# Count tiles of a graph convolution built in two row tiles of the TensorE array, two slots at a time

## The reference, cut to what matters

```python
deg_out = jnp.maximum(jax.ops.segment_sum(ones, src, num_segments=N), 1.0)
deg_in = jnp.maximum(jax.ops.segment_sum(ones, dst, num_segments=N), 1.0)
h = x * jax.lax.rsqrt(deg_out)[:, None]
agg = jax.ops.segment_sum(h[src], dst, num_segments=N)
h = agg * jax.lax.rsqrt(deg_in)[:, None]
h = jax.nn.relu(h @ W + b)
gnn = h / jnp.maximum(jnp.linalg.norm(h, axis=1, keepdims=True), EPS)
x = x + gnn + mix(xn)
x = x + ffn(layernorm(x))      # 8 experts, top 1, capacity 1.25
```

## Time and profile before

| | us |
|---|---|
| median of 3 runs | 1531.53 (1530.54 to 1535.5) |
| the profiled execution | 1529.9 |
| its span in the trace | 1528.7 |
| TensorE busy | 1394.8 |
| VectorE busy | 1304.5 |
| ScalarE busy | 925.8 |
| GpSimd busy | 709.4 |

### The profile page before, as it was taken

One profiled execution on the slowest core, in us unless ns is written; L12 is line 12 of the kernel. 1 busy time (PEld: TensorE's weight loads), 2 busy tenths in 40 slices (PEclk: granted clock), 3 DMA queues, 4 the chain that ended last, 5 costly groups with the idle time before them and its releaser, 6 DMA issues. The chain is left out here.

```text
span 1528.7 us, 37659 instructions
## 1 busy us (share of the span) xinstructions
PE 1394.8 (91%) x11633; PEld 970.7 (63%) x11634; DVE 1304.5 (85%) x2630; ACT 925.8 (61%) x2090; POOL 709.4 (46%) x740
## 2 busy tenths in 40 slices
PE   3899999896889999999999999999996699899985
PEld 3666666674546666666666666666664588889985
DVE  7999998899768999999999999999995577857774
ACT  4456655567446667666666666666663566555653
POOL 4578776506212443244323442244321567776575
PEclk9899999998899999999999999999998799999998
DMA  9011111000001100011111100110113333243220
GB/s 295 30 33 41 40 39 37 29 21 28 2 4 50 54 34 34 34 69 34 34 34 61 42 34 34 36 67 34 34 35 130 121 109 120 95 136 105 82 69 17
DMA packets 61417, 89.46 MB, mean 59 GB/s; under 512 B 10411, under 2 KB 40749, under 8 KB 61312
## 3 DMA queue, kind: packets, MB, share of 16 engines
q1 hardware_dynamic: 49999, 67.18, 13.0%
q0 software_dynamic: 11328, 21.23, 4.9%
HBM read 62.89 MB, written 35.01 MB: 64 GB/s over the span
## 5 line engine op out<-in xcount | busy, mean ns | idle before, releaser
L1453 PE MATMUL bank<-reg_b,reg_a 128*128 128x512 f16 x2401 | 637.5, 379 | 0.7 <-ACT reg_a L1087 0.7
L1087 ACT ACTIVATE reg_a<-bank 128x392 f16<-128x392 f32 x784 | 370.4, 496 | 219.9 <-PE bank L1447 218.5
L1662 DVE TENSOR_TENSOR reg_c<-iota_v,reg_c 128x2048 f16<-128x2048 f16 (+2 forms) x398 | 422.9, 1085 | 30.3 <-PE bank L1447 22.9
L782 POOL COPY key_deg<-deg_k 128x1 f32 (+1 forms) x49 | 93.8, 1914 | 463.2 <-DVE reg_c L1793 463.2
L1447 PEld LDWEIGHTS bank<-reg_a,reg_c 128*128 128x128 f16 x3136 | 214.5, 99 | 144.5 <-issue 11.4
L1447 PE MATMUL bank<-reg_a,reg_c 128*128 128x98 f16 x3136 | 262.6, 209 | 8.5 <-issue 5.3
L1453 PEld LDWEIGHTS bank<-reg_b,reg_a 128*128 128x128 f16 x2401 | 194.1, 97 | 117.4 <-issue 2.0
L1662 DVE TENSOR_TENSOR reg_a<-iota_h,reg_c 128x1568 f16<-128x1568 f16 x196 | 214.9, 1096 | 0.0
L1343 PE MATMUL bank<-reg_w,xnT_t 128*128 128x512 f16 x588 | 137.3, 383 | 3.4 <-DVE xnT_t L1734 2.4
L1619 PE MATMUL bank<-w_hi,hid_hi 128*128 128x256 f32 (+1 forms) x368 | 108.6, 295 | 11.5 <-DVE w_lo L2138 5.4
L1282 PE MATMUL bank<-reg_c 128*64 128x98 f16 x1616 | 92.8, 212 | 16.1 <-DVE reg_c L1662 9.0
(11 more groups left out here) (343 smaller groups left out, 2665.8 us busy)
## 6 DMA issues: line engine op xcount, KB each, us to landing
reg_b<-in_L_ffn_w SPq DMA_DIRECT2D x16, 1024.0 KB
tok_rows<-reg_e SPq DMA_DIRECT2D x24, 512.0 KB, 3.8
xnT_rows<-xnT_t SPq DMA_DIRECT2D x25, 256.0 KB
x_t<-in_x SPq DMA_DIRECT2D x24, 256.0 KB
xnT_t<-xnT_rows SPq DMA_DIRECT2D x24, 256.0 KB, 2.9
out<-reg_e SPq DMA_DIRECT2D x24, 256.0 KB
reg_a<-in_x SPq DMA_DIRECT2D x1, 3072.0 KB, 24.1
reg_a<-in_x SPq DMA_DIRECT2D x1, 2560.0 KB, 14.6
```

The source lines that it names most:

```text
L782: g.tensor_copy(key_deg[:, :], deg_k[:, ds(b, 1)])
L1087: return a.activation(AT[k].rearrange("p h (w t) -> p h w t", w=2)[:, :, :, s * GROUP:(s + 1) * GROUP], tile_ps[bk][:, 0:GROUP * 2 * NB].r ...
L1453: ins = t_.matmul(agg_ps[k][:, :], AT[k][:, h, :], h_all[:, h, :], start=(first and h == 0), stop=False)
L1662: return v_.tensor_tensor(out.rearrange("p t (v u) -> p t v u", u=2), iota.rearrange("p (v u) -> p v u", u=2).unsqueeze(1).to_broadcast(sh ...
```

## The change

`build` now makes one node's tile: it takes 64 partitions (lower or upper, by the parity of the slot) of both operands and 49 columns of high marks. A matmul thus covers 64 rows of the array; even slots use rows 0 to 63, odd slots rows 64 to 127. GROUP becomes 8 (8 x 49 = 392 columns, as before), SLOTS stays 16, and a block has 128 count matmuls instead of 64. Slots are built in pairs: one wait for both banks, then 16 matmuls that alternate between the two row tiles and the two banks. The sums of both slots come behind. `iota_h` and its two instructions go; the high marks have 50 columns instead of 98 in both halves. The evacuation copies 8 tiles of 49 into 8 neighbouring places. The wait for `bd_set` in block 0 stands at the end of slot 1 instead of slot 2.

```diff
-GROUP = 4
-SLOTS = TILES // GROUP
+GROUP = 8
+SLOTS = P // GROUP
+CG = SLOTS // CHUNKS
...
         def tile_evac(k, s, bk):
-            return a.activation(AT[k].rearrange("p h (w t) -> p h w t", w=2)[:, :, :, s * GROUP:(s + 1) * GROUP],
-                                tile_ps[bk][:, 0:GROUP * 2 * NB].rearrange("p (t w h) -> p h w t", w=2, t=GROUP), ACT.Copy)
+            first = s % 2 * TILES + s // 2 * GROUP
+            return a.activation(AT[k][:, :, first:first + GROUP],
+                                tile_ps[bk][:, 0:GROUP * NB].rearrange("p (t h) -> p h t", t=GROUP), ACT.Copy)
...
         def prepare(b, s):
-            if (b, s) == (0, 2):
+            if (b, s) == (0, 1):
                 pe.wait_ge(mix_prep, MIX["bd_set"])
...
-        def build(c, s, bk):
-            for i in range(GROUP):
-                ins = t_.matmul(tile_ps[bk][:, i * 2 * NB:(i + 1) * 2 * NB], lo_ring[c][:, s % CG * GROUP + i, :],
-                                hi_ring[c][:, s % CG * GROUP + i, :], start=True, stop=True)
-            return ins
+        def build(c, s, bk, i):
+            half = slice(s % 2 * SLOT, (s % 2 + 1) * SLOT)
+            t = s % CG // 2 * GROUP + i
+            return t_.matmul(tile_ps[bk][:, i * NB:(i + 1) * NB], lo_ring[c][half, t, :], hi_ring[c][half, t, 0:NB],
+                             start=True, stop=True)
...
-                pe.wait_ge(tile_out, b * SLOTS + (s + 1))
-                apart(pe)
-                build(s // CG, s, s % len(tile_ps)).then_inc(tile_ready, 1)
+                if s % 2 == 0:
+                    pe.wait_ge(tile_out, b * SLOTS + (s + 2))
+                    apart(pe)
+                    for i in range(GROUP):
+                        for w in range(2):
+                            ins = build(s // CG, s + w, (s + w) % len(tile_ps), i)
+                            if i == GROUP - 1:
+                                ins.then_inc(tile_ready, 1)
...
-        def block_iota():
-            v_.tensor_copy(iota_h[0:64, :], iota_v[0:64, 0:2 * NB])
-            v_.tensor_scalar(iota_h[64:P, :], iota_v[64:P, 0:2 * NB], -float(NB), None, ALU.add
-                             ).then_inc(base_set, 1)
...
-            return marks(hi_ring[ring], iota_h[:, :], kT[k][:, 1, g0:g0 + CHUNK, :], ALU.is_equal)
+            return marks(hi_ring[ring], iota_v[:, 0:NBE], kT[k][:, 1, g0:g0 + CHUNK, :], ALU.is_equal)
```

More of the change, by code:

```diff
@@ L52 @@
 CHUNK = 16
-CG = CHUNK // 4
 CHUNKS = TILES // CHUNK
-GROUP = 4
-SLOTS = TILES // GROUP
+GROUP = 8
+SLOTS = P // GROUP
+CG = SLOTS // CHUNKS
 RING = 4
@@ L144, in build @@
     AT = [reg_a[:, k * ATN:(k + 1) * ATN].bitcast(F16).rearrange("p (h d) -> p h d", h=NB) for k in range(2)]
-    HIN, LON = CHUNK * 2 * NB // 2, CHUNK * P // 2
+    HIN, LON = CHUNK * NBE // 2, CHUNK * P // 2
     o = 2 * ATN
@@ L234, in build @@
     iota_v = sb("iota_v", [P, P], F16)
-    iota_h = sb("iota_h", [P, 2 * NB], F16)
     iota_k = sb("iota_k", [P, SLOT])
@@ L1468, in work @@
                     apart(pe)
-                    build(RING, s, 0).then_inc(x_tile, 1)
+                    for i in range(GROUP):
+                        ins = build(RING, s, 0, i)
+                    ins.then_inc(x_tile, 1)
                 pe.wait_ge(x_tile_out, r * SLOTS + SLOTS)
@@ L1806, in degrees @@
                 v_.tensor_copy(hist_sb[:, :], hist_ps).then_inc(hist_out, 1)
-            if k == 1:
-                block_iota()
             if k == 2:
@@ L1823, in keys_begin @@
             key_halves(0)
-            dve.wait_ge(base_set, 4)
+            dve.wait_ge(base_set, 3)
             dve.wait_ge(consts, 19)
@@ L1914, in work @@
                     marks(lo_ring[RING], iota_v[:, :], x_kT[:, 0, g0:g0 + CHUNK, :], ALU.is_equal)
-                    marks(hi_ring[RING], iota_h[:, :], x_kT[:, 1, g0:g0 + CHUNK, :], ALU.is_equal).then_inc(x_tiles, 1)
+                    marks(hi_ring[RING], iota_v[:, 0:NBE], x_kT[:, 1, g0:g0 + CHUNK, :], ALU.is_equal).then_inc(x_tiles, 1)
             more_rounds(dve, rounds, work)
```

## The result

The changed kernel takes 1551.79 us (median of 4 runs, 1549.11 to 1554.31) against 1533.51 us for the kernel before in runs beside it. The ratio is 1.0119, interval 1.0096 to 1.0141: slower by some 18 us. The forecast was +13 us, a ratio of 1.0088.

The account below looks back on a forecast made before the run. It took TensorE's sequence of starts as the bound: (1.73 + 1.47 - 2.91) x 48 = 13.9 us more, less 1 us, is 13 us, added to 1531.5 for 1545 us; the 8-in-10 range was 1528 to 1622.

Parts of the forecast that it names:

- What bounds the kernel: Steady block loop: TensorE's sequence of starts is the time in 48 of 49 blocks, 31.05 us a pair.
- a nanosecond there is one in the result: Steady blocks: any time added or saved on TensorE shows fully in the result; on VectorE it does not.
- "free change" rival: Count groups: changing the array's rows costs nothing, giving 1474 us; chance 0.16, shared with a half-free change at 1509.
- Part 1: Count matmuls: two in different row tiles run together, a pair every 27 ns, 1.73 us a block instead of 2.91.
- Part 2: Array shape changes around count groups: about 0.21 us a group for entering and leaving, 1.47 us a block.
- the 0.03 us for the second matmul: After shape changes: the second matmul of a new shape is late as well, together 0.03 us a group.
- Part 3: Order of slots built in pairs: banks are free in time, 2.6 us of lateness covered, so no cost.
- The step "nothing" for block 0: Block 0: moving the wait for the key-value matrix from slot 2 to slot 1's end costs nothing.
- Part 4: VectorE's high marks: 1.09 to 0.61 us each, 94 us less busy time, off the steady path; 1 us gained early.
- The 110 x 800 row: VectorE: the profile row taken as the time of a narrowed high mark, 0.61 us.
- The lead of 1 us ahead of block 0: Ahead of block 0, where TensorE waited 5.2 us for VectorE: shorter marks save 1 us, between 0 and 2.

Follow-up runs that it names:

- before_full_close: The kernel before, with each block's closing matmul using 128 rows of zeros instead of one row: 1528.29 us, ratio 0.9963 to the kernel before.
- four_groups_wide: The changed kernel with four count groups a block, moved key transposes, 128-row closing matmul and 98-column high marks: 1503.55 us, ratio 0.9952 to the kernel before.
- wide_marks: The changed kernel with high marks 98 columns wide again, of which the matmuls read 49: 1548.45 us, ratio 1.0105 to the kernel before.
- after_again: The changed kernel run once more, nothing altered, 10 runs: 1543.86 us, ratio 1.0078 to the kernel before.
- the short rounds: The changed kernel with half the count matmuls left out in extra-round code this graph never runs: 1517.53 us, ratio 1.0051 to the kernel before.
- serial_tiles: The changed kernel with each group's eight lower-tile count matmuls issued first, then all eight upper: 1580.28 us, ratio 1.0356 to the kernel before.

## Why the prediction was right, and where its steps were off
**What bounds the kernel: right for a longer TensorE, too strong for a shorter one.** The pair grew by what TensorE's starts grew, with no wait. But "a nanosecond there is one in the result" holds upward only; before_full_close and four_groups_wide show VectorE's bound at about 31.1 us, the very period of the kernel before. This would not have moved this forecast, but it means that the "free change" rival, 1474 us, could not have come from TensorE alone: it would have needed the narrow marks too, which the sum books at 1 us. No run went so far down: the shortest steady pair is 29.88 us.

**Part 1: right.** 26 ns a pair, predicted 27; the two of a pair 3 to 4 ns apart. The column tiles of the key transposes were the right row to go by. By the Trainium skill (TensorE: Matmul & The Clock Gate, Measured speedup vs the span model), tiles start about 4 ns apart; these rows agree.

**Part 2: right.** A whole group was booked at 8 x 27 + 210 = 426 ns; the starts give (312 - 215) + 308 + (227 - 215) = 417. The visit itself has 97 ns at entry, 93 at exit and 12 at the second sum, 0.20 us together, predicted 0.21; and 0.17 to 0.18 us when the number of visits is changed. The fp32 rows of 64 rows and the f16 row of one row stood for f16 matmuls of 64 rows to within 10 ns at entry and exit; the 0.03 us for the second matmul was 0.012. Per pair of blocks: predicted +0.58 us, measured +0.51.

**Part 3: right in the steady part, not at the start.** No bank wait there, no cost of the order. The step "nothing" for block 0 failed. The moved wait itself is longer, 1.50 us instead of 1.00, but blocks 0 and 1 together take 5.2 us less. Of that, 1.3 us are the stop at z0, which the changed kernel doesn't have, some 2 us seem to be the marks' (wide_marks), and about 2 us are as much as two profiles of the old order differ by.

**Part 4: right that it is off the path, wrong in size and place.** The 110 x 800 row was a fair measure of a mark by itself: 0.57 us against 0.61. The error is in what it was taken from. The 1.09 us of the kernel before is a mean over 0.97 us and the few marks that GpSimd delays by about 1.07 us, and that delay stays with the shorter mark. So a mark saves 0.40 us, not 0.48, and 80 us went, not 94. The lead of 1 us ahead of block 0 isn't there: TensorE waits 5.4 us for the same instruction (now L1764), as in the earlier trace rows.

**What was left out: block 2.** It takes 6.8 us more, in the main for an early stop of 3 us at "issue", 1 us more of stop at its end, and a stretch at half clock. In the sum this and the gain of blocks 0 and 1 nearly cancel: 11.3 - 5.2 + 6.8 = +12.9 us from the start of block 0 to the last sum, against the 13 of the forecast. That it matches so closely is luck. The other 8 us of the first pair of profiles lie ahead of block 0 and are variation; after_again (+11 us) has little of it. With the short rounds the kernel is 7.6 us slower by its medians, and the stages of its profile give 11.4 - 5.7 + 1.4 - 0.8 = +6.3.

## What to carry to other kernels
Before small matmuls are packed into row tiles, count how often the array changes its shape: each visit cost 0.17 to 0.2 us here, as much as four 98-column matmuls, so the packing paid with 32 small matmuls a visit and not with 16. Look for shape changes that are there already, one-row or half-array helpers among them, and put new ones beside them. When TensorE is at 100% and VectorE at 95%, a cut on TensorE is worth only the distance between the two periods, unless VectorE is cut with it.

## What the runs showed of the hardware
- The pace of about 25 ns between small matmuls belongs to each row tile. Two tiles fed in turn give a pair every 26 ns; fed one after the other, the second begins while the first still has three of eight to start.
- A change from 128 rows to 64 rows in f16 costs 97 ns, the way back 93 (and 12 ns at the second matmul after it); in fp32 it is 90 each way. To one row it costs 96 ns and back 77, so one small helper of one row and two columns cost 0.17 us a block.
- TensorE stops for 1 to 5 us at "issue" in the first blocks, most often near code that it skips and at the start of the loop over pairs; in the steady blocks no such stop was seen. With twice the count matmuls in the skipped code an early stop of 3 us came in addition, and with half of them left out again it went. Where it was followed by 6.8 us of half clock the block took 23.0 us, and in serial_tiles, at full clock, 21.3.
- A VectorE instruction on 128 x 800 f16 elements takes 0.57 us and about 1.64 beside GpSimd's 128 x 512 one (L835); one on 128 x 1568 takes 0.97 and 2.04.
